# Each indirect row transfer waits for the one before it, and three pairs of a scatter move behind the group norm's root

## The chip, the cores and the metric

One core of one Trainium2 chip. The metric is device microseconds of one execution. Before the change it is 2342.63 us, the median of 3 runs (2340.99 to 2352.11).

## The reference, cut to what matters

Eight images of 128 channels by 32 by 32 (1024 tokens of 128 channels each) go through four layers, each added to its input:

```
x = x + deform_conv(_gn(x))               # layer 0: 3x3 deformable convolution
x = x + attention_conv(_gn(x))            # layer 1: softmax attention over 1024 positions
t = tokens(x)
t = t + attention(_ln_t(t))               # layer 2: softmax attention with a distance bias
t = t + top2_experts(_ln_t(t), weights a) # 8 experts, hidden 256, each token uses 2
t = t + linear_attention(_ln_t(t))        # layer 3
t = t + top2_experts(_ln_t(t), weights b)
```

`_gn` is a group norm over 4 channels and all positions, `_ln_t` a layer norm over a token's 128 channels; both divide by a square root. The expert layer adds, for each token, the outputs of its two best experts with their shares.

## The kernel before, in words

Five engines run programs that are written out image by image. While image p is in its convolution and its two attentions, the expert layers and layer 3 of images p-1, p-2 and p-3 are woven in at numbered hooks; tables such as `SEND_A_AT` give the hook of every step. The hooks of the convolution and of the short stage behind it are numbered 0 to 52 (`G_HOOKS`), those of the two attentions start again at 0 (`X_HOOKS`). An engine runs its own list strictly in order and waits on semaphores, so on GpSimd, which does nothing but small work, a table decides only what stands before what.

The expert layer of an image works on sorted rows. After routing, GpSimd **scatters** the 1024 normed tokens twice (first and second choice) into `xs` in device memory: 16 indirect transfers (`MOVES`), each of 128 rows of 512 bytes, out of `tnF` (first expert layer, l = 0) or `tnB` (second, l = 1). `send(m, l, part)` issues two of them. SyncE's `first_blocks` asks for the first six weight blocks, then waits until all 16 have landed (`sent0` or `sent1`, 256 counts an image) and loads `xs` into `blocks_sb` in three pieces (L689). TensorE turns these blocks over four at a time (L1101, step 0 of `experts`), works through 23 blocks, and SyncE stores the results to `ys`. Then GpSimd **gathers** them back in 16 indirect transfers into `gotten` (`fetch`), and VectorE's `settle` (L1829), which waits for all 16 (`got0` or `got1`), adds them to the tokens.

GpSimd also takes every norm's root (`rsqrt`, `rsqrt_half`: variance to the power -0.5). Each sits between a VectorE step that makes the variance and one that uses the root: `gn0` and `gn1` are the group norms before the convolution and before the first attention, `ln2` the norm before the second attention, `lnf2` and `lnf3` those before the expert layers, `ln3` that before layer 3. `ln2`, `lnf2` and `lnf3` go in two halves of four token tiles. One larger piece, the sum `tokD + tnB` at L785, is GpSimd's too.

So in one period GpSimd's list holds, in this order: the gather of l = 0 for image p-1; the `ln3` root and half a `lnf2` root; four transfers of the gather of l = 1 for image p-3, the other `lnf2` half, L785, and the other twelve; the scatter of l = 0 for image p-1, the `lnf3` halves and the `gn1` root among it; the scatter of l = 1 for image p-2 with the first `ln2` half ahead of its last two transfers. After the last image's convolution there is a tail of hooks with the same steps and nothing else to weave them into; there the last image's expert layers are computed densely, without transfers.

Of the kernel before, what the change touches and what calls it, by code (L numbers as in the profile page):

```python
# [73 lines left out]
def placed(first, at, hooks):  # L74

    return [[first + n for n, h in enumerate(at) if h == hook] for hook in range(hooks)]
# [23 lines left out]
LAYER3_PLACES = placed(EARLY_LAYER3, LAYER3_AT, G_HOOKS)  # L100
GATE_A_AT = [1, 4, 4, 4, 7, 8, 8, 10, 13, 17, 17, 21, 21, 22]
GATE_A_PLACES = placed(EARLY_GATING, GATE_A_AT, G_HOOKS)
SEND_A_AT = [28, 32, 34, 34, 36, 36, 44, 44]
SEND_A_PLACES = placed(0, SEND_A_AT, G_HOOKS)
GATE_B_AT = [36, 42, 43, 43, 45, 46, 46, 46, 46, 51, 51]
GATE_B_PLACES = placed(0, GATE_B_AT, G_HOOKS)
# [171 lines left out]
def at(m, k, c):  # L278

    reg, off = m  # L280
    return off * k + c if reg is None else reg * k + (off * k + c)


def later(value):

    return not isinstance(value, int) or value > 0
# [12 lines left out]
def build(nc, x, sel_in, count_in, early_in, late_in, wa_in, wb_in, out):  # L299
# [3 lines left out]
    with ExitStack() as ctx:  # L303
# [5 lines left out]
        def sem(name):  # L309
            if name not in sems:  # L310
                sems[name] = ctx.enter_context(nc.semaphore(name))
            return sems[name]
# [52 lines left out]
        got = [gotten[:, r * N:(r + 1) * N].rearrange("p (a b) -> p a b", a=NT) for r in range(2)]  # L365
# [89 lines left out]
        def which(l):  # L455

            return ("lnf2", "lnf3")[l], "ab"[l], "FB"[l], (tnF, tnB)[l], (tnTA, tnTB)[l]

        def nth(m, l, k, c):

            i, v = m
            if l == 0:
                return c if i is None and v == 0 else at(m, 2 * k, c - k)
            return at(m, 2 * k, c + 2 * k if v + 1 < B - 1 else c + k)

        def before_this(m, l, k):

            i, c = m
            if l == 0:
                return at(m, k, -k)  # L470
            return at(m, k, 2 * k) if c + 1 < B - 1 else (B - 1) * k
# [7 lines left out]
        def there(p, n):  # L479

            return not isinstance(p, int) or 0 <= p - n < B
# [23 lines left out]
        def tail_side(rear, layer3, gating, send, first_blocks, experts, fetch, settle, load, dense):  # L505

            def side(n):
                for (thread, l, age), places in TAIL_PLACES.items():
                    m = None, B - 1 - age
                    for step in places[n]:  # L510
                        if thread == "rear":
                            rear(m, step)
                        elif thread == "layer3":
                            layer3(m, step)
                        elif thread == "gating":
                            gating(m, l, step)
                        elif thread == "send":
                            send(m, l, step)
                        elif thread == "first":
                            first_blocks(m, l)  # L520
                        elif thread == "experts":
                            experts(m, l, step)
                        elif thread == "fetch":
                            fetch(m, l, step)
                        elif thread == "settle":
                            settle(m, l, step)
                        elif thread == "load":
                            load(l)
                        else:
                            dense(m, l, step)  # L530
            return side
# [46 lines left out]
        def periods(period, tail):  # L578

            for p in range(B):  # L580
                period((None, p), p)
            for n in range(X_HOOKS, TAIL_HOOKS):
                tail(n)
# [169 lines left out]
        @block.gpsimd  # L753
        def _(pool):
            pool.memset(mhalf[:, :], -0.5).then_inc(sem("mhalf_set"), 1)
            pool.memset(prob[:, :], 0.0)
            pool.drain().then_inc(sem("prob_zero"), 1)
            pool.memset(xrows[:, :], 0.0)
            pool.drain().then_inc(sem("pads_zero"), 1)
            pool.wait_ge(sem("mhalf_set"), 1)  # L760

            def rsqrt_half(m, w, name, h):
                pool.wait_ge(sem(name + "_var"), at(m, 2, h + 1))
                cols = slice(4 * h, 4 * h + 4)
                pool.tensor_tensor(stat[w]["rstd"][:, cols], stat[w]["var"][:, cols], mhalf[:, cols],
                                   ALU.pow).then_inc(sem(name + "_rstd"), 1)

            def rsqrt(m, w, name, width):
                pool.wait_ge(sem(name + "_var"), at(m, 1, 1))
                pool.tensor_tensor(stat[w]["rstd"][:, 0:width], stat[w]["var"][:, 0:width], mhalf[:, 0:width],  # L770
                                   ALU.pow).then_inc(sem(name + "_rstd"), 1)

            def gating(m, l, step):
                name, f, w, tn, tnT = which(l)
                for h in range(2):
                    if step == GATE_AT[h][POWER]:
                        rsqrt_half(m, w, name, h)

            def layer3(m, step):
                if step == 2:  # L780
                    rsqrt(m, "B", "ln3", NT)
                elif step == 7:

                    pool.wait_ge(sem("ln3_tn"), at(m, 2, 2))
                    pool.tensor_tensor(tokD[:, :, :], tokD[:, :, :], tnB[:, :, :], ALU.add).then_inc(sem("tok3_res"), 1)  # L785

            MOVES = [(r, j) for r in range(2) for j in range(NT)]

            def send(m, l, part):

                if part == 0:
                    pool.wait_ge(sem(f"routed{l}"), at(m, 1, 1))
                    pool.sem_inc(sem("moves_begun"), 1)
                tn = which(l)[3]
                for r, j in MOVES[2 * part:2 * part + 2]:
                    pool.indirect_dma_start(xs[l], bass.IndirectOffsetOnAxis(row[l][r][:, j:j + 1], 0), tn[:, j, :], None)\  # L796
                        .then_inc(sem(f"sent{l}"), 16)

            def fetch(m, l, part):

                if part == 0:
                    if later(before_this(m, l, 1)):
                        pool.wait_ge(sem(f"settled{1 - l}"), before_this(m, l, 1))
                    for y in range(STORES):
                        pool.wait_ge(sem(f"ys_out{y}"), 16 * nth(m, l, 2, 2))
                    pool.sem_inc(sem("moves_begun"), 1)
                for r, j in MOVES[2 * part:2 * part + 2]:
                    pool.indirect_dma_start(got[r][:, j, :], None, ys[l], bass.IndirectOffsetOnAxis(row[l][r][:, j:j + 1], 0))\  # L808
                        .then_inc(sem(f"got{l}"), 16)

            def rear(m, step):
                if step < MOVE_STEPS:
                    fetch(m, 1, step)

            def start(m, step):
                if step == 5:
                    rsqrt(m, "S", "gn0", 1)

            tail = tail_side(rear, layer3, gating, send, nothing, nothing, fetch, nothing, nothing, nothing)

            def period(m, p):
                side = g_sides(m, p, rear, layer3, gating, send, nothing, nothing)
                for n in range(G_HOOKS):
                    if there(p, 0) and n == CONV_HOOKS + 5:
                        rsqrt(m, "F", "gn1", 1)
                    side(n)
                side = x_sides(m, p, layer3, gating, send, nothing, nothing, fetch, nothing, start, tail)
                for n in range(X_HOOKS):
                    if there(p, 0) and n in (ATTENTION_HOOKS - 5, ATTENTION_HOOKS + 4):
                        rsqrt_half(m, "F", "ln2", n // ATTENTION_HOOKS)  # L830
                    side(n)

            rsqrt((None, 0), "S", "gn0", 1)
            pool.wait_ge(sem("xs_zero"), 64)


            periods(period, tail)
# [1329 lines left out]
```

## Time and profile before

| | |
|---|---|
| median of 3 runs | 2342.63 us |
| span of the profiled execution | 2532.1 us |
| TensorE busy | 1926.7 us, 76% |
| VectorE busy | 1494.0 us, 59% |
| ScalarE busy | 1039.0 us, 41% |
| GpSimd busy | 555.5 us, 22%, 535 instructions, 448 of them indirect transfers |

The profiled execution is known by its span alone, the time from its first to its last instruction; it is 8% above the median of the runs. The rows quoted further down are times within it, so what is summed there has to be brought to the scale of the runs by 2342.63 / 2532.1 = 0.925. A transfer's own instruction on GpSimd ends when its descriptors are written, not when its rows have landed.

### The profile page before, as it was taken

To read this page: it belongs to the slowest core of one execution; us is meant where nothing else is said; L and a number is where in the kernel's file an instruction comes from. 1 tells how busy PE (TensorE), PEld (TensorE's weight loads), DVE (VectorE), ACT (ScalarE), POOL (GpSimd) and SP (SyncE) were. 2 spreads that over 40 slices of the span, in tenths; PEclk is the share of its full clock that TensorE was granted. 3 is DMA by queue.
4 is the path that set the end of the run, shared out by engine and by line. 5 is a ranking of instruction groups with operands and counts; after the bars stand their busy time and mean duration, and the time that the engine had idled before them with its cause. 6 is when DMAs were issued, how large, how long until landed. Compare 5 with 4: busy or idle time off the path is not lost.

```text
span 2532.1 us, 35891 instructions
## 1 busy us (share of the span) xinstructions
PE 1926.7 (76%) x10992; PEld 1518.5 (60%) x10992; DVE 1494.0 (59%) x3449; ACT 1039.0 (41%) x1773; POOL 555.5 (22%) x535
## 2 busy tenths in 40 slices
PE   4777878887688777877778876786778877768749
PEld 1665656566556565756646665565656666556636
DVE  2356545876357754777447763577547864485363
ACT  3134144525363162733546253642627335443323
POOL 0000112021213323032222312133230422232020
PEclk7889989988899889988889888998889988888969
DMA  7901952474446734584455844476344844431410
GB/s 250 198 1 42 210 150 76 110 170 136 123 137 162 199 101 127 146 184 142 117 145 158 187 138 122 135 178 182 101 132 146 192 132 126 128 122 55 129 35 9
DMA packets 259912, 337.51 MB, mean 133 GB/s; under 512 B 29552, under 2 KB 191840, under 8 KB 259424
## 3 DMA queue, kind: packets, MB, share of 16 engines
q1 hardware_dynamic: 243648, 297.70, 44.7%
q0 software_dynamic: 14336, 29.39, 4.2%
q10 hardware_dynamic: 1696, 7.66, 0.8%
q8 instruction: 105, 1.72, 0.3%
q14 instruction: 127, 1.04, 0.1%
HBM read 267.56 MB, written 67.08 MB: 132 GB/s over the span
## 4 chain that ended last, share of the span: by engine, by line
PE 33%; issue 19%; DVE 18%; ACT 6%; DVEq 5%; DMA 5%; SPq 4%; another core or an unknown queue 4%; POOL 3%; ACTq 2%; PEld 0%; PEldq 0%; POOLq 0%
PE pair L948 5%; PE pair L1067 4%; POOL gotten L808 2%; PE pair L935 2%; PE pair L1235 2%; PE pair L1225 2%; PE pair L1115 2%; DMA dist<-hats 2%; PE pair L1127 2%; PE pair L1075 2%; DVE dist L1642 2%; PE pair L861 2%; PE pair L881 2%; DVE nmax L1751 1%
## 5 line engine op out<-in xcount | busy, mean ns | idle before, releaser
L948 PE MATMUL pair<-dist,thirds 128*128 128x256 f32 (+6 forms) x1440 | 299.2, 360 | 66.7 <-DVE dist L1642 60.7
L948 PEld LDWEIGHTS pair<-dist,thirds 128*128 128x128 f32 x1440 | 259.5, 205 | 115.3 <-DVE dist L1642 61.2
L1067 PE MATMUL pair<-vt,dist 128*128 128x128 f32 x2048 | 270.7, 288 | 37.3 <-DVEq L1745 32.9
L1067 PEld LDWEIGHTS pair<-vt,dist 128*128 128x128 f32 x2048 | 256.2, 202 | 60.5 <-DVEq L1745 49.8
L1433 ACT ACTIVATE hidden_sb<-pair,wring 128x128 f32<-128x128 f32 x644 | 184.3, 367 | 234.8 <-PE pair L1115 135.2
L808 POOL DMA_INDIRECT gotten<-ys,row x224 | 226.0, 1009 | 128.1 <-issue 65.8
L1115 PE MATMUL pair<-turned_sb,wring 128*128 128x128 f32 x1288 | 193.1, 295 | 65.1 <-DVEq L1796 37.2
L1127 PE MATMUL pair<-wring,hidden_sb 128*128 128x128 f32 x1288 | 184.5, 288 | 71.6 <-DVE tnF L1764 35.9
L1115 PEld LDWEIGHTS pair<-turned_sb,wring 128*128 128x128 f32 x1288 | 172.8, 205 | 106.6 <-DVEq L1796 61.9
L1642 DVE TENSOR_TENSOR dist<-dist,prob 128x1024 f32<-128x1024 f32 x144 | 173.9, 1224 | 95.7 <-DMA dist<-hats 46.9
L1127 PEld LDWEIGHTS pair<-wring,hidden_sb 128*128 128x128 f32 x1288 | 169.3, 202 | 81.7 <-issue 65.8
L1751 DVE TENSOR_REDUCE nmax<-pair 128x1 f32<-128x1024 f32 x128 | 156.6, 1224 | 50.0 <-PE pair L1075 35.0
L796 POOL DMA_INDIRECT xs<-tnB,row x112 | 108.9, 973 | 322.6 <-DVEq L1927 290.1
L796 POOL DMA_INDIRECT xs<-tnF,row x112 | 126.5, 1130 | 236.9 <-DVEq L1927 164.1
L1405 ACT ACTIVATE prob<-pair,nmax 128x1024 f32<-128x1024 f32 x128 | 142.4, 1113 | 83.7 <-DVE nmax L1751 73.0
L1340 ACT ACTIVATE thirds<-pair 128x768 f32<-128x768 f32 x96 | 77.8, 810 | 239.1 <-PE pair L935 220.9
L935 PE MATMUL pair<-early_sb,xrows 128*128 128x384 f32 x384 | 152.7, 522 | 24.1 <-ACT thirds L1340 15.4
L1059 PE MATMUL pair<-early_sb,prob 128*128 128x128 f32 x1024 | 150.6, 280 | 20.0 <-ACT hidden_sb L1433 7.7
L1808 DVE TENSOR_TENSOR by<-pair,wring 128x256 f32<-128x256 f32 x168 | 69.2, 412 | 160.3 <-PE pair L1127 79.3
L1393 ACT ACTIVATE dist<-pair 128x512 f32<-128x512 f32 x128 | 76.3, 596 | 168.0 <-PE pair L1059 98.9
L1059 PEld LDWEIGHTS pair<-early_sb,prob 128*128 128x128 f32 x1024 | 122.0, 145 | 33.7 <-issue 12.2
L1075 PE MATMUL pair<-qk 128*128 128x512 f32 x256 | 130.2, 634 | 9.6 <-issue 6.1
(256 smaller groups left out, 3162.0 us busy)
## 6 DMA issues: line engine op xcount, KB each, us to landing
dist<-hats SPq DMA_DIRECT2D x576, 128.0 KB
wring<-wa SPq DMA_DIRECT2D x161, 321.0 KB
wring<-wb SPq DMA_DIRECT2D x161, 321.0 KB
prob<-hats SPq DMA_DIRECT2D x288, 128.0 KB
hats<-dist SPq DMA_DIRECT2D x40, 512.0 KB, 3.9
ys<-by SPq DMA_DIRECT2D x70, 256.0 KB, 2.3
blocks_sb<-xs SPq DMA_DIRECT2D x28, 512.0 KB, 6.7
blocks_sb<-xs SPq DMA_DIRECT2D x14, 448.0 KB, 8.0
```

What stands on the lines that cost most here:

```text
L796: pool.indirect_dma_start(xs[l], bass.IndirectOffsetOnAxis(row[l][r][:, j:j + 1], 0), tn[:, j, :], None)\
L808: pool.indirect_dma_start(got[r][:, j, :], None, ys[l], bass.IndirectOffsetOnAxis(row[l][r][:, j:j + 1], 0))\
L935: last = pe.matmul(pair[1][:, 512 * c:512 * c + 384], xn[:, (2 * d + c) * P:(2 * d + c + 1) * P], const("w0")[:, t * 384:(t + 1) * 384], s ...
L948: last = pe.matmul(pair[0][:, a:b], z[k // 3 % 2][:, c, k % 3, :], rhs(a, b), start=bank not in opened, stop=final, skip_group_check=True)
L1059: last = pe.transpose(psum[bank][:, t * P:(t + 1) * P], pr[j % 3][:, (4 * h + t) * P:(4 * h + t + 1) * P], ident)
L1067: last = pe.matmul(psum[bank][:, 0:P], prT[j % 2][:, t, :], vt[:, t, :], start=(t == 0), stop=(t == NT - 1))
L1075: last = pe.matmul(pair[j % 2][:, h * 512:(h + 1) * 512], queries[:, j * P:(j + 1) * P], keys[:, h * 512:(h + 1) * 512], start=True, stop= ...
L1115: last = pe.matmul(psum[bank][:, to:to + P], wring[:, r, h * P:(h + 1) * P], bT[b0 // 4 % 2][:, (b % 4) * P:(b % 4 + 1) * P], start=True, ...
L1127: last = pe.matmul(psum[bank][:, to:to + P], hid[b % 4][:, h * P:(h + 1) * P], wring[:, b % RINGW, W2_AT + h * C:W2_AT + (h + 1) * C], sta ...
L1433: last = act.activation(hid[b % 4][:, h * P:(h + 1) * P], psum[bank][:, of:of + P], ACT.Gelu, bias=wring[:, b % RINGW, B1_AT + h:B1_AT + h ...
L1642: dve.tensor_tensor(slot, slot, windows(k, half), ALU.mult).then_inc(sem("hat_ready"), 1)
L1751: dve.tensor_reduce(nmax[:, j:j + 1], pair[j % 2][:, :], AX.X, ALU.max, negate=True)\
```

## The change

Every indirect transfer but the first of a batch of 16 gets a wait: for all 16 counts of every transfer issued before it in its batch. The wait is carried by the transfer's own instruction. Nothing else is computed or moved, but the table `SEND_A_AT` puts the last three pairs of the scatter of l = 0 at hooks 46, 47 and 48 where they had 36, 44 and 44; the `gn1` root stands at hook 45.

```diff
-SEND_A_AT = [28, 32, 34, 34, 36, 36, 44, 44]
+SEND_A_AT = [28, 32, 34, 34, 36, 46, 47, 48]
...
-                for r, j in MOVES[2 * part:2 * part + 2]:
+                for n, (r, j) in enumerate(MOVES[2 * part:2 * part + 2]):
+                    if part or n:
+
+                        pool.wait_ge(sem(f"sent{l}"), at(m, 256, 32 * part + 16 * n))
                     pool.indirect_dma_start(xs[l], bass.IndirectOffsetOnAxis(row[l][r][:, j:j + 1], 0), tn[:, j, :], None)\
                         .then_inc(sem(f"sent{l}"), 16)
...
-                for r, j in MOVES[2 * part:2 * part + 2]:
+                for n, (r, j) in enumerate(MOVES[2 * part:2 * part + 2]):
+                    if part or n:
+
+                        pool.wait_ge(sem(f"got{l}"), at(m, 256, 32 * part + 16 * n))
                     pool.indirect_dma_start(got[r][:, j, :], None, ys[l], bass.IndirectOffsetOnAxis(row[l][r][:, j:j + 1], 0))\
                         .then_inc(sem(f"got{l}"), 16)
```

Only GpSimd's list changes. Its rows for the end of a convolution, before (`xs<-tnF` is the scatter of l = 0, `xs<-tnB` that of l = 1; xN is a run of N equal rows):

```order
L796 DMA xs<-tnF,row 2944x128 [waits routed0]
L796 DMA xs<-tnF,row 2944x128 x11
L765 TENSOR_TENSOR rstdB<-varB,mhalf 128x4 [waits lnf3_var]
L796 DMA xs<-tnF,row 2944x128 x4
L770 TENSOR_TENSOR rstdF<-varF,mhalf 128x1 [waits gn1_var]
L765 TENSOR_TENSOR rstdB<-varB,mhalf 128x4 [waits lnf3_var]
L796 DMA xs<-tnB,row 2944x128 [waits routed1]
```

And the same place in the changed kernel:

```order
L799 DMA xs<-tnF,row 2944x128 [waits routed0]
L799 DMA xs<-tnF,row 2944x128 [waits sent0] x9
L765 TENSOR_TENSOR rstdB<-varB,mhalf 128x4 [waits lnf3_var]
L770 TENSOR_TENSOR rstdF<-varF,mhalf 128x1 [waits gn1_var]
L765 TENSOR_TENSOR rstdB<-varB,mhalf 128x4 [waits lnf3_var]
L799 DMA xs<-tnF,row 2944x128 [waits sent0] x6
L799 DMA xs<-tnB,row 2944x128 [waits routed1]
```

Two of the twelve scatters ahead of the first `lnf3` half and the four ahead of the `gn1` root now stand behind both, and, since the second `lnf3` half comes right after the `gn1` root, behind that too.

GpSimd's rows for the start of a convolution, where the gather of l = 1 begins (`-` before, `+` changed):

```order
 L765 TENSOR_TENSOR rstdF<-varF,mhalf 128x4 [waits lnf2_var]
-L808 DMA gotten<-ys,row 128x128 [waits ys_out2,ys_out1,settled0,ys_out0]
-L808 DMA gotten<-ys,row 128x128 x3
+L814 DMA gotten<-ys,row 128x128 [waits ys_out2,ys_out1,settled0,ys_out0]
+L814 DMA gotten<-ys,row 128x128 [waits got1] x3
 L765 TENSOR_TENSOR rstdF<-varF,mhalf 128x4 [waits lnf2_var]
 L785 TENSOR_TENSOR tokD<-tokD,tnB 128x1024 [waits ln3_tn]
-L808 DMA gotten<-ys,row 128x128 x12
```

Here nothing changes places: the second `lnf2` half and the sum at L785 stand behind four transfers as before, and three of these four now wait.

## Rows read from the trace of the kernel before

**Rows 1.** The page: engines, their busy time, share of the span and instructions.
```profile
PE 1926.7 (76%) x10992; PEld 1518.5 (60%) x10992; DVE 1494.0 (59%) x3449; ACT 1039.0 (41%) x1773; POOL 555.5 (22%) x535
```
**Rows 2.** Timeline of POOL, fifth period: start, length, operation [idle before, releaser].
```profile
1136.20 1.44 POOL L796 DMA_INDIRECT xs<-tnF,row  x1 [30.43 <-DVEq L1927]
...
1152.39 0.97 POOL L796 DMA_INDIRECT xs<-tnF,row  x1 [0.30 <-issue]
1161.65 1.03 POOL L765 TENSOR_TENSOR rstdB<-varB,mhalf 128x4 f32<-128x4 f32 x1 [8.29 <-DVE varB L1692]
...
1171.20 0.57 POOL L770 TENSOR_TENSOR rstdF<-varF,mhalf 128x1 f32<-128x1 f32 x1 [3.47 <-DVEq L1575]
1174.43 1.01 POOL L765 TENSOR_TENSOR rstdB<-varB,mhalf 128x4 f32<-128x4 f32 x1 [2.66 <-DVE varB L1692]
```
**Rows 3.** Timeline of SP (issues of transfers): the fifth period, and the tail.
```profile
1173.85 3.92 SPq L689 DMA_DIRECT2D blocks_sb<-xs  x3
...
2344.46 2.18 SPq L689 DMA_DIRECT2D blocks_sb<-xs  x3
```
**Rows 4.** Timeline of PE, the same place of the fifth period.
```profile
1187.03 0.60 PE L1101 MATMUL pair<-early_sb,blocks_sb 128*128 128x128 f32 x4
```
**Rows 5.** The tile blocks_sb: its loads, from issue to landing, in us.
```profile
DMA to landing us min/median/max: 3.9/7.2/9.2
```
**Rows 6.** DMA queues in 2342.15:2344.15, 1301.3:1303.6 and 1376.2:1385.5: packets, MB, share.
```profile
q0 software_dynamic: 64, 0.13, 19.5%
...
q0 software_dynamic: 64, 0.13, 22.8%
...
q0 software_dynamic: 128, 0.26, 14.1%
```
**Rows 7.** Timeline of DVE: four instructions that make or use what POOL waits for.
```profile
1135.01 0.34 DVE L1926 TENSOR_REDUCE row<-picked 128x8 int32<-128x64 f32 x2
...
1256.99 0.17 DVE L1692 TENSOR_SCALAR varF<-mvF 128x4 f32<-128x4 f32 x1
...
1260.19 0.16 DVE L1701 SCALAR_TENSOR_TENSOR nmrF<-mvF,rstdF 128x4 f32<-128x4 f32 x1
...
1385.64 2.33 DVE L1701 SCALAR_TENSOR_TENSOR nmrF<-mvF,rstdF 128x4 f32<-128x4 f32 x1
```
**Rows 8.** Timeline of POOL: the first ln2 root, fifth period and last image.
```profile
1257.25 1.04 POOL L765 TENSOR_TENSOR rstdF<-varF,mhalf 128x4 f32<-128x4 f32 x1 [21.59 <-DVE varF L1692]
...
2138.53 1.04 POOL L765 TENSOR_TENSOR rstdF<-varF,mhalf 128x4 f32<-128x4 f32 x1 [11.34 <-DVE varF L1692]
```
**Rows 9.** Timeline of POOL: the gather of l = 1 begins, then the second lnf2 root.
```profile
1376.23 1.01 POOL L808 DMA_INDIRECT gotten<-ys,row  x1 [0.18 <-issue]
...
1384.59 1.02 POOL L765 TENSOR_TENSOR rstdF<-varF,mhalf 128x4 f32<-128x4 f32 x1 [3.51 <-DVE varF L1692]
```
**Rows 10.** Timeline of POOL: the first transfer of four more gathers.
```profile
418.51 1.03 POOL L808 DMA_INDIRECT gotten<-ys,row  x1 [0.18 <-issue]
...
1281.42 1.03 POOL L808 DMA_INDIRECT gotten<-ys,row  x1 [9.14 <-DMA ys<-by]
...
2244.90 1.12 POOL L808 DMA_INDIRECT gotten<-ys,row  x1 [0.18 <-issue]
...
2414.53 1.03 POOL L808 DMA_INDIRECT gotten<-ys,row  x1 [11.24 <-DMA ys<-by]
```
**Rows 11.** Timeline of DVE: the first use of each of these four gathers.
```profile
448.17 0.61 DVE L1829 SCALAR_TENSOR_TENSOR tokD<-gotten,share,tokD 128x128 f32<-128x128 f32 x2
...
1325.07 0.61 DVE L1829 SCALAR_TENSOR_TENSOR tokD<-gotten,share,tokD 128x128 f32<-128x128 f32 x2 [0.21 <-issue]
...
2277.39 1.72 DVE L1829 SCALAR_TENSOR_TENSOR tokC<-gotten,share,tokC 128x128 f32<-128x128 f32 x5
...
2442.78 0.35 DVE L1829 SCALAR_TENSOR_TENSOR xc<-gotten,share,xc 128x128 f32<-128x128 f32 x1
```
**Rows 12.** Groups of DVE: line, operation, count | busy, mean ns | idle before, releasers.
```profile
L1642 DVE TENSOR_TENSOR dist<-dist,prob 128x1024 f32<-128x1024 f32 x144 | 173.9, 1224 | 95.7 <-DMA dist<-hats 46.9 <-DMA prob<-hats 38.2 <-issue 8.1
```

## The prediction

> **What bounds the kernel now.** The page's first part comes first: TensorE is busy for 76% of the span and no engine comes near all of it [rows 1], so the kernel is bound by the order in which in-order engines hand work to each other, and a wait costs what it holds up. GpSimd is idle for most of the span; its load is not the question, but what stands behind its transfers is. So I read its timeline, and for each batch of 16 transfers looked for the next thing that needs it. Three things are to be seen there. A scatter goes out every 1.27 us (0.97 us long after 0.30 us idle) and GpSimd then idles 8.29 us before the first `lnf3` root, so its transfers are paid for by nobody [rows 2]. Behind the scatter of l = 0 the slack is small: SyncE issues the loads of `blocks_sb` at 1173.85 [rows 3] and TensorE turns the first block over at 1187.03 [rows 4], of which the load takes 3.9 us at best [rows 5]. And most gathers have room: one begins at 1281.42 [rows 10] and is first used at 1325.07 [rows 11].
>
> **What one waited transfer costs.** It takes the landing of the one before plus the wake of GpSimd.
>
> The landing, with the DMA engines otherwise idle: a window of 2.0 us that begins with the issue of a batch's last scatter holds all 64 packets of the last two transfers, 0.13 MB [rows 6], and SyncE, which waits for this landing, goes on at 2344.46 [rows 3]: 1.9 us, and 0.4 us for SyncE's start. The same for a gather: a window of 2.3 us, 2.2 us taken. Beside other loads: the four gathers from 1376.2 have all 128 packets moved by 1385.5, 9.3 us [rows 6]. One alone lies between 9.3 / 4 = 2.3 us and 9.3 - 3 x 1.3 = 5.4 us; I take 3.7 us, near the middle. For scatters beside some load I take 2.3 us.
>
> The wake does not show, since no transfer carries a wait today. Bound from below: a norm's root, which carries its own wait, starts 0.09 us after the variance is made (1256.99 + 0.17 [rows 7] to 1257.25 [rows 8]). Bound from above: a batch's first transfer stands behind an instruction that only waits and counts, and starts 0.85 us after routing's last write (1135.01 + 0.34 [rows 7] to 1136.20 [rows 2]). Nearest in kind is the 0.30 us between two transfers, same engine and operation; with 0.07 us more for the semaphore I take 0.37 us. A waited transfer then costs 2.27 us (scatter, idle), 2.67 us (scatter, some load), 2.57 us (gather, idle) or 4.07 us (gather, loaded), against 1.27 us.
>
> On the wake the Trainium skill has a rule (Perfetto Trace Analysis, DMA Instruction — SWDGE (GPSIMD)): such an instruction is decoded first, sits in a wait queue, and moves to the processors once its semaphores are satisfied, so a wait that it carries costs no decoding afterwards. By that rule the wake is near the lower bound and the sum is that of the first rival below; no row here shows it for a transfer.
>
> **The change part by part, in us of the profiled execution.**
>
> 1. Scatter of l = 0, seven periods. The `gn1` root at 1171.20 and the second `lnf3` root, which ends at 1174.43 + 1.01 [rows 2], keep their places, 4.24 us apart; 0.2 us later six scatters start where the four before them had gone out already. They land 5 x 2.27 + 1.9 = 13.25 us on, SyncE starts 0.4 us later and the first piece takes 3.9 us (DMA is idle by then): 4.24 + 0.2 + 13.25 + 0.4 + 3.9 = 22.0 us behind the `gn1` root, against 15.83 us for TensorE's first turn now (1187.03 - 1171.20). TensorE is in order, VectorE and ScalarE wait for that block: **6.2 us late, 43 us in seven periods**. With the median landing of 7.2 us [rows 5] it would be 23 us more. That the last three pairs come behind the root is what keeps the `gn1` root on time: the ten scatters ahead of it have 1171.20 - 1136.20 = 35.0 us, enough up to (35.0 - 2.4) / 9 = 3.6 us each.
>
> 2. Scatter of l = 1. Thirteen waits lie ahead of the first `ln2` root: 13 x (2.67 - 1.27) = 18.2 us. GpSimd idles 21.59 us there now [rows 8], so it is hidden, in all images but the last, whose idle time is 11.34 us [rows 8]. VectorE reads the root 1.9 us after it is there (1260.19 [rows 7] against 1257.25 + 1.04): 18.2 - 11.3 - 1.9, **5 us once**.
>
> 3. Gather of l = 0. It lasts 15 x 2.57 + 2.2 = 40.8 us. The room is 43.65 us (1281.42 [rows 10] to 1325.07 [rows 11]), in six periods about the same: hidden, with 2.9 us left. In the first it is 29.66 us (418.51 to 448.17 [rows 10, 11]): **11 us once**.
>
> 4. Gather of l = 1, five periods. Three waits stand ahead of the second `lnf2` root: 3 x (4.07 - 1.3) = 8.3 us, against 3.51 us idle [rows 9]. VectorE takes that root the moment it ends (1384.59 + 1.02, then 1385.64 [rows 7]), so it is 4.8 us late. But this is where the convolution starts, in which VectorE waits for loads, 46.9 + 38.2 us in all, 10.6 us an image [rows 12]; loads that go on while it is held shorten those waits. Between nothing and all I take half: 2.4 x 5, **12 us**. The other twelve have the whole convolution.
>
> 5. Tail. Here nothing is woven in and the engines work in chains. The gather at 2244.90 takes fifteen waits, three of them loaded, with a root (1.0) and the L785 sum (2.3, as long as VectorE's 1385.64 beside it [rows 7]) in between: 3 x 4.07 + 12 x 2.57 + 2.2 + 3.3 = 48.6 us, to 2293.5, used now at 2277.39: 16 us. The last one, 40.8 us from 2414.53, ends at 2455.3 and is used now at 2442.78 [rows 10, 11]: 12.5 us; two `lnf3` roots and the last image's last layer follow it. **28.5 us.**
>
> Sum: 43 + 5 + 11 + 12 + 28.5 = 99.5 us on a span of 2532.1 us. The runs are shorter by the factor 0.925, so 92 us on the median of 2342.63: **2435 us**.
>
> **The rivals.**
>
> *Short wake* (0.09 us, 0.28 us less a transfer; the Trainium skill's rule above stands behind it). Parts 1 to 5 fall to 34, 1.4, 7, 10 and 20: 72 us, times 0.925 = 67, **2409 us**. For it speaks the root's 0.09 us; against it the constant 0.30 us between transfers.
>
> *Long wake* (0.85 us, 0.48 us more). Part 1 gives 60; part 2 11 in the last image and 0.9 in five others; part 3 18 in the first period and 7.2 - 2.9 = 4.3 in six others, half of it counted since TensorE has queued work in the second attention, so 31; part 4 16; part 5 43: 166 us, times 0.925 = 153, **2496 us**. For it speaks the only transfer in the trace that follows a wait.
>
> *Overrun.* If scatters beside the convolution's loads cost as much as gathers there, 3.7 + 0.85 us, they pass the 3.6 us of part 1 and the `gn1` root is 9 x 0.95 = 8.6 us late in six periods, 51 us more; with the halves of parts 3 and 4 counted whole (28 us): 245 us, times 0.925, **2569 us**.
>
> *Hidden.* The waits cost nothing if the six scatters behind the root land in time: (1187.03 - 3.9 - 0.4 - 1175.64 - 1.9) / 5 = 1.04 us each, less than a landing [rows 6] and even than today's 1.27 us. It could be only if runs without a profiler land far faster: **2343 us**.
>
> *Faster.* Twelve scatters now go out in 17 us beside the loads VectorE waits for in the convolution [rows 12]; ten spread out, and six behind it, leave these loads more room. If that halves the waits (42.5 us) and part 1 is hidden as above: 2342.63 - 39 = **2303 us**. It decides only where a waited scatter costs at most 1.04 us.
>
> **How the numbers follow.** A measurement of this kernel tells about 0.5% from no change. Forecast (wake 0.37 us) 0.47, long wake 0.26, short wake 0.16, overrun 0.05, hidden 0.04, faster 0.02. Slower is the sum of the first four, 0.94; same 0.04, faster 0.02. The range goes from under the short wake's time, 2385 us (absorption as in part 4 may reach part 1 too), to the long wake's, 2500 us; outside are overrun, hidden, faster and some of the edges, less than 2 in 10.
>
> **What would show it.** In the changed profile a scatter should start every 2.3 to 2.7 us and a gather every 2.6 to 4.1 us, with idle time ended by a landing; the first L1101 rows (there L1107) should lie 22 us behind the `gn1` root and be waited for; the `gn1` root's own wait should be no longer than now; L1829 (there L1835) should wait for `gotten` in the first period and twice in the tail. I am wrong if the starts lie 2.0 or 2.8 us apart (the wake), if TensorE's first turn is not held up, or if the convolution gives back more than half of what the `lnf2` root loses.

## The result, and the profile after

The changed kernel takes 2786.7 us (median of 4 runs, 2774.07 to 2798.88), and the kernel before took 2345.07 us beside it (4 runs): a ratio of 1.189, 95% interval 1.185 to 1.193. That is 442 us slower, against 92 us forecast and an upper end of 2500 us. The direction was right, the size was not.

The page of the changed kernel: the engines' busy time, the row of the queue of indirect transfers (packets, MB, share), and the chain that ended last.

```profile
PE 1925.9 (69%) x10992; PEld 1518.1 (55%) x10992; DVE 1495.2 (54%) x3449; ACT 1039.8 (37%) x1773; POOL 558.9 (20%) x535
...
q0 software_dynamic: 14336, 29.39, 3.8%
...
DMA 49%; issue 17%; PE 14%; DVE 8%; SPq 3%; POOL 3%; ACT 2%; DVEq 2%; ACTq 1%; PEld 0%; POOLq 0%; PEldq 0%
DMA gotten<-ys,row 25%; DMA xs<-tnF,row 11%; DMA xs<-tnB,row 9%; PE pair L1073 2%; PE pair L1121 2%; PE pair L1241 1%; PE pair L1231 1%; DMA blocks_sb<-xs 1%; DMA ys<-by 1%; PE pair L954 1%; DMA prob<-hats 1%; DVE nmax L1757 1%; DVE dist L1750 1%; PE pair L941 1%; PE pair L1081 1%
```

Every engine runs the same instructions as before [rows 1], and the span is longer. That TensorE's busy time equals the one in [rows 1] is no sign that its speed is unchanged: the second profile of the unchanged kernel, further down, has 1876.3 us for the same 10992 matmuls, at a mean granted clock of 0.907 against 0.849 here and 0.883 in the first. The clock has two levels in these traces, 2.4 GHz (1.00) and 1.2 GHz (0.50). At the turn of the first block below, behind 8.65 us without work, the four matmuls run at 0.50 and take 1.11 us, against 0.60 us at 1.00 in [rows 4]. So the waits also made TensorE's own work 50 us longer; no run holds the clock fixed, so what part of the loss this is stays open.

The chain is half DMA, and 25 + 11 + 9 = 45% of the span are landings of indirect transfers, on a queue that moves data for 3.8% of it. So the loss comes from latency, not from bandwidth.

Who waits is in the view of waits: engine, tile and line <- releaser: us in total, times, longest.

```profile
POOL gotten L814 <- DMA gotten<-ys,row: 522.7, 203, 7.4
...
POOL xs L799 <- DMA xs<-tnF,row: 208.7, 98, 7.0
...
POOL xs L799 <- DMA xs<-tnB,row: 195.1, 104, 4.8
...
DVE tokD L1835 <- DMA gotten<-ys,row: 137.3, 7, 24.4
DVE nmrF L1707 <- POOL rstdF L765: 130.1, 26, 18.6
...
PE pair L1107 <- DMA blocks_sb<-xs: 77.6, 8, 19.6
...
DVE tokC L1835 <- DMA gotten<-ys,row: 56.4, 6, 16.4
...
DVE dist L1648 <- DMA prob<-hats: 45.0, 17, 4.7
...
DVE dist L1648 <- DMA dist<-hats: 40.4, 26, 12.6
...
DVE xc L1835 <- DMA gotten<-ys,row: 21.1, 1, 21.1
...
DVE nmrB L1707 <- POOL rstdB L765: 15.6, 7, 5.6
DVE nmrF L1584 <- POOL rstdF L770: 15.2, 8, 10.1
```

GpSimd's own waits (first three rows, 926 us) are not the loss by themselves; it is only 442 us. What costs are three waits of the others: VectorE's for `gotten` (137.3 + 56.4 + 21.1 = 214.8 us), VectorE's for a root behind the transfers (the `nmr` rows), and TensorE's for `blocks_sb` (77.6 us). The waits for the `hats` loads are as in [rows 12], so the loads gave nothing back there.

The timeline of GpSimd in the period that answers to [rows 2, 8, 10]: the end of a scatter of l = 0, a scatter of l = 1 with its `ln2` root, and the gather of l = 0.

```profile
1261.36 0.97 POOL L799 DMA_INDIRECT xs<-tnF,row  x1 [2.37 <-DMA xs<-tnF,row]
1262.36 1.04 POOL L765 TENSOR_TENSOR rstdB<-varB,mhalf 128x4 f32<-128x4 f32 x1
1265.19 0.56 POOL L770 TENSOR_TENSOR rstdF<-varF,mhalf 128x1 f32<-128x1 f32 x1 [1.79 <-DVEq L1581]
...
1269.60 1.03 POOL L799 DMA_INDIRECT xs<-tnF,row  x1 [0.19 <-issue]
...
1284.02 0.96 POOL L799 DMA_INDIRECT xs<-tnF,row  x1 [1.56 <-DMA xs<-tnF,row]
...
1320.73 0.96 POOL L799 DMA_INDIRECT xs<-tnB,row  x1 [35.76 <-DVEq L1933]
...
1358.72 0.96 POOL L799 DMA_INDIRECT xs<-tnB,row  x1 [1.54 <-DMA xs<-tnB,row]
1361.21 0.96 POOL L799 DMA_INDIRECT xs<-tnB,row  x1 [1.54 <-DMA xs<-tnB,row]
1362.20 1.03 POOL L765 TENSOR_TENSOR rstdF<-varF,mhalf 128x4 f32<-128x4 f32 x1
...
1384.15 1.03 POOL L814 DMA_INDIRECT gotten<-ys,row  x1 [6.83 <-DMA ys<-by]
...
1433.20 0.94 POOL L814 DMA_INDIRECT gotten<-ys,row  x1 [1.89 <-DMA gotten<-ys,row]
```

The view of the chain tells landing and wake apart (start, length, what; "issue" is the time from the landing to the start that waited for it), at the end of that scatter of l = 1, and between the last landing of the scatter of l = 0 and SyncE:

```profile
1356.23 2.23 DMA xs<-tnB,row
1358.45 0.27 issue
...
1286.27 0.02 issue
```

Three readings. The price of a waited transfer: on a quiet queue scatters start 2.49 us apart (1358.72 to 1361.21), of which 2.23 are the landing and 0.27 the wake. The forecast had 1.9 and 0.37. It had split what it saw wrongly: it set 0.4 us aside for SyncE's start, and SyncE starts 0.02 us behind the landing. The idle time ahead of the `ln2` root, 21.59 us in [rows 8], is gone: the root starts the moment its engine is done with the thirteenth waited scatter. And the gather of l = 0 takes 49.05 us from its first start to its last, 3.27 us a step on the average.

SyncE's timeline behind the scatter of l = 0 (compare [rows 3]):

```profile
1286.29 1.95 SPq L689 DMA_DIRECT2D blocks_sb<-xs  x3
```

TensorE's, there and behind the tail's scatter of l = 1 (compare [rows 4]):

```profile
1290.44 1.11 PE L1107 MATMUL pair<-early_sb,blocks_sb 128*128 128x128 f32 x4 [8.65 <-DMA blocks_sb<-xs]
...
2596.32 1.11 PE L1107 MATMUL pair<-early_sb,blocks_sb 128*128 128x128 f32 x4 [19.60 <-DMA blocks_sb<-xs]
```

VectorE's uses of the first `ln2` root, and of the second `lnf2` root of the next convolution (compare [rows 7]):

```profile
1363.26 0.16 DVE L1707 SCALAR_TENSOR_TENSOR nmrF<-mvF,rstdF 128x4 f32<-128x4 f32 x1 [14.07 <-POOL rstdF L765]
...
1499.52 2.31 DVE L1707 SCALAR_TENSOR_TENSOR nmrF<-mvF,rstdF 128x4 f32<-128x4 f32 x1 [4.77 <-POOL rstdF L765]
```

From the start of a scatter's last transfer until SyncE goes on it takes 2.27 us (1284.02 to 1286.29), as forecast (1.9 + 0.4), though nearly all of it is landing. The waits in which the forecast saw nothing are those of 14.07 us (scatter of l = 1) and of about 20 us for `tokD` (gather of l = 0, 137.3 us in seven).

### The profile page after: what moved, and what is told of

It is laid out like the page before. It is cut to its first block, busy times and chain, and to the rows that moved or that the text cites. A ratio compares the mean times of both kernels' runs of the same rounds, so it can differ in the third digit from the quotient of the medians.

```text
span 2784.9 us, 35891 instructions
## 1 busy us (share of the span) xinstructions
PE 1925.9 (69%) x10992; PEld 1518.1 (55%) x10992; DVE 1495.2 (54%) x3449; ACT 1039.8 (37%) x1773; POOL 558.9 (20%) x535
## 3 DMA queue, kind: packets, MB, share of 16 engines
q0 software_dynamic: 14336, 29.39, 3.8%
q8 instruction: 105, 1.72, 0.3%
## 4 chain that ended last, share of the span: by engine, by line
DMA 49%; issue 17%; PE 14%; DVE 8%; SPq 3%; POOL 3%; ACT 2%; DVEq 2%; ACTq 1%; PEld 0%; POOLq 0%; PEldq 0%
DMA gotten<-ys,row 25%; DMA xs<-tnF,row 11%; DMA xs<-tnB,row 9%; PE pair L1073 2%; PE pair L1121 2%; PE pair L1241 1%; PE pair L1231 1%; DMA blocks_sb<-xs 1%; DMA ys<-by 1%; PE pair L954 1%; DMA prob<-hats 1%; DVE nmax L1757 1%; DVE dist L1750 1%; PE pair L941 1%; PE pair L1081 1%
## 5 line engine op out<-in xcount | busy, mean ns | idle before, releaser
L954 PE MATMUL pair<-dist,thirds 128*128 128x256 f32 (+6 forms) x1440 | 305.3, 364 | 82.3 <-DVE dist L1648 76.0
L954 PEld LDWEIGHTS pair<-dist,thirds 128*128 128x128 f32 x1440 | 263.2, 207 | 137.3 <-DVE dist L1648 80.5
L1073 PEld LDWEIGHTS pair<-vt,dist 128*128 128x128 f32 x2048 | 262.0, 206 | 57.2 <-DVEq L1751 45.0
L1133 PE MATMUL pair<-wring,hidden_sb 128*128 128x128 f32 x1288 | 174.5, 279 | 26.6 <-DVE tokA L1772 24.6
L1133 PEld LDWEIGHTS pair<-wring,hidden_sb 128*128 128x128 f32 x1288 | 161.4, 195 | 32.7 <-issue 27.7
L901 PE MATMUL pair<-early_sb,tnF 128*128 128x128 f32 x192 | 36.8, 323 | 138.4 <-DVEq L1711 138.4
```

What stands on the lines that cost most here:

```text
L954: last = pe.matmul(pair[0][:, a:b], z[k // 3 % 2][:, c, k % 3, :], rhs(a, b), start=bank not in opened, stop=final, skip_group_check=True)
L1073: last = pe.matmul(psum[bank][:, 0:P], prT[j % 2][:, t, :], vt[:, t, :], start=(t == 0), stop=(t == NT - 1))
L1133: last = pe.matmul(psum[bank][:, to:to + P], hid[b % 4][:, h * P:(h + 1) * P], wring[:, b % RINGW, W2_AT + h * C:W2_AT + (h + 1) * C], sta ...
```

## The experiments

Two theories were at hand. **A**: the rooms that the prediction read for the scatter of l = 1 and the gather of l = 0 belonged to the one profiled execution, whose span lay 8% above the runs, and are much smaller in an ordinary one; the loss is then the sum of the three waits above, batch by batch. **B**: the rooms are there, and something else costs, the moved pairs or each wait as such.

**The kernel before, unchanged, profiled again.**

> The kernel before, unchanged, profiled a second time. The profiled execution of before had a span of 2532.1 us against 2343 us for its runs, and in it all three compute engines stand still together five times for 9 to 12 us while a scatter of l = 1 is issued and three times for 4 to 6 us during a gather of l = 0. Theory A (standstills of that one execution, absent from the runs): span near 2345 us, no such standstill, and the room of a gather of l = 0 (first transfer to first use) near 33 us instead of 43.65 us, that of the scatter of l = 1 ahead of the ln2 root near 29 us instead of 39.15 us. Theory B (the profiler stops the engines whenever 14 to 16 transfers go out back to back): span near 2530 us again, standstills at the same places. Theory C (the standstills belong to the kernel and the runs have them too): the span and the runs of this call agree near 2530 us.

2343.17 us, ratio 1.001 (0.998 to 1.004); the profiled span is 2337.8 us. GpSimd's timeline in the same place as above:

```profile
1156.48 1.03 POOL L796 DMA_INDIRECT xs<-tnB,row  x1 [42.88 <-DVEq L1927]
...
1173.09 0.97 POOL L796 DMA_INDIRECT xs<-tnB,row  x1 [0.30 <-issue]
1181.62 1.04 POOL L765 TENSOR_TENSOR rstdF<-varF,mhalf 128x4 f32<-128x4 f32 x1 [7.56 <-DVE varF L1692]
...
1206.02 1.03 POOL L808 DMA_INDIRECT gotten<-ys,row  x1 [9.37 <-DMA ys<-by]
...
1288.60 1.01 POOL L808 DMA_INDIRECT gotten<-ys,row  x1 [0.18 <-issue]
```

VectorE's use of that root, and its first uses of the gathers of l = 0 and of l = 1:

```profile
1184.56 0.17 DVE L1701 SCALAR_TENSOR_TENSOR nmrF<-mvF,rstdF 128x4 f32<-128x4 f32 x1
...
1237.42 0.61 DVE L1829 SCALAR_TENSOR_TENSOR tokD<-gotten,share,tokD 128x128 f32<-128x128 f32 x2 [0.20 <-issue]
...
1345.08 1.98 DVE L1829 SCALAR_TENSOR_TENSOR tokC<-gotten,share,tokC 128x128 f32<-128x128 f32 x6
```

Here the idle time ahead of the root is 7.56 us, not 21.59, and the room of the gather is 1237.42 - 1206.02 = 31.4 us, not 43.65. Its view of waits has VectorE wait 26.3 us for roots, most of it in this row:

```profile
DVE nmrF L1701 <- POOL rstdF L765: 18.3, 15, 2.3
```

The first profile had the difference as standstills of all three computing engines in just these places: set side by side instruction by instruction, VectorE's timelines of the two profiles differ by 194 us at the end, and about 175 of them arise beside a scatter of l = 1 or a gather of l = 0. Its windows view (length, busy time and count of TensorE, its weight loads, VectorE, ScalarE and GpSimd, clock, DMA share, GB/s) there:

```profile
1226.00:1238.00 12.00, 0.36 (x1) 0.19 (x1) 0.00 (x0) 0.00 (x0) 7.53 (x8) 0.63 0.37 110
```

VectorE's timeline at the ends of two such stretches:

```profile
1238.10 0.16 DVE L1761 RECIPROCAL rinv<-rsum 128x1 f32<-128x1 f32 x1 [13.80 <-remote]
...
1303.20 0.42 DVE L1808 TENSOR_TENSOR by<-pair,wring 128x256 f32<-128x256 f32 x1 [12.86 <-remote]
```

In 12 us GpSimd started eight scatters while TensorE, VectorE and ScalarE together ran one matmul and its weight load. The releaser reads "remote": nothing that the profile records ended the wait. The second standstill, before 1303.20, lies within the gather of l = 0. A standstill gives the batch under way time in which nothing that needs it comes nearer; the second profile has no stretch of over 3 us without work on these three engines, but for the loads at its start. Theory A holds for the rooms. The expectation's other two are out: a profile does not always hold standstills, and the runs, at 2343 us, do not have them.

**The move alone, and the waits alone.** The order of pairs without the waits, and the waits with the order of before:

```diff
-SEND_A_AT = [28, 32, 34, 34, 36, 36, 44, 44]
+SEND_A_AT = [28, 32, 34, 34, 36, 46, 47, 48]
```

> Kernel before with the table of the change alone (three pairs of the scatter of l = 0 behind the gn1 root), no waits. Theory A (the loss is the waits): six transfers 1.27 us apart behind the second lnf3 root land about 8.3 us after it, TensorE's first turn is 0 to 2 us late in seven periods, less than four transfers' time earlier: between 2335 and 2360 us. Rival (the move itself holds up the blocks): 40 us or more, 2385 us.

2356.65 us, ratio 1.005 (1.003 to 1.008): 13 us. The waits view has one new row for it:

```profile
PE pair L1101 <- DMA blocks_sb<-xs: 10.8, 6, 2.9
```

> The changed kernel with the old table: every transfer waits, and the last four scatters of l = 0 stand ahead of the gn1 root. Theory A: twelve, then four waited scatters at 2.5 to 3 us each hold the first lnf3 root and the gn1 root up by 5 to 15 us, while the blocks land earlier behind the root; what is lost ahead of the root is about what is won behind it: 2760 to 2830 us. Rival (the move is what costs): under 2700 us.

2816.18 us (2 runs), ratio 1.202 (1.195 to 1.210), 29 us more than the changed kernel. Both runs came out in theory A's range. So the table costs 13 us by itself, and given the waits it saves about 30: it takes six waited scatters from ahead of the `gn1` root (VectorE's wait for that root is 74.2 us with the old table and 15.2 with the new), two of them from ahead of the first `lnf3` root (56.6 and 15.6 us).

**One batch at a time.** The changed kernel with waits in one kind of batch only; the first is shown, in the other three the condition stands on the other l or in `fetch`:

```diff
-                    if part or n:
+                    back_ = 2 * part + n - 1
+                    if back_ >= 0 and (l == 0):
-                        pool.wait_ge(sem(f"sent{l}"), at(m, 256, 32 * part + 16 * n))
+                        pool.wait_ge(sem(f"sent{l}"), at(m, 256, 16 * back_ + 16))
```

> Edit: the changed kernel with the waits in the scatter of l = 0 alone; the new table stays. Theory A (the waits cost what TensorE, VectorE and the loads are seen to wait for in the changed kernel's trace, batch by batch): TensorE's seven waits for blocks_sb are 7.1 to 9.2 us, 58 us together, and the table by itself costs 12: 2343 + 70 = 2413 us (2400 to 2425). Theory B (the sums of the prediction, with the slack read in the profile of before that had standstills): 43 x 0.925 + 12 = 52, 2395 us. The two are near each other here, because no slack of a standstill goes into this part.

2438.07 us, ratio 1.044 (1.040 to 1.048), +97 us.

> Edit: waits in the scatter of l = 1 alone; the new table stays. Theory A: in an undisturbed run of before GpSimd idles 7.6 us ahead of the first ln2 root, not 21.6, and thirteen waits lengthen what lies ahead of it by 24 us, so the root is late by 12 to 14 us in each of six periods, and TensorE waits 19.6 us in the tail: about 101 us and 12 for the table, 2456 us (2435 to 2465). Theory B (hidden but in the last image, 5 us): 2343 + 5 + 12 = 2360 us.

2477.84 us, ratio 1.059 (1.055 to 1.063), +137 us.

> Edit: waits in the gather of l = 0 alone; the new table stays. Theory A: the room is 31 us, not 43.65, and the waited batch takes 51, so VectorE waits 18 to 24 us for gotten in each of seven periods, 137 us together, of which 86 are time in which TensorE and ScalarE stand still too: 86 to 137 and 12 for the table, 2441 to 2492 us. Theory B (hidden but in the first period, 11 us): 2343 + 10 + 12 = 2365 us, up to 2373 with the longer wake that was measured.

2498.08 us, ratio 1.067 (1.062 to 1.071), +157 us.

> Edit: waits in the gather of l = 1 alone; the new table stays. Theory A: VectorE waits 7 to 9 us for gotten in five periods, 40 us, then 16.5 and 21.1 in the tail, and the second lnf2 root is 4.8 us late five times: about 100 us and 12 for the table, 2455 us (2435 to 2465). Theory B (parts 4 and 5 as predicted, 40.5 x 0.925, and no wait for gotten in the five periods): 2343 + 37 + 12 = 2392 us. If the four parts add up, the four runs less four times the table are 429 us, what the changed kernel has over the table; if waits of one batch take the place of another's, the four give more than that.

2468.62 us, ratio 1.054 (1.049 to 1.059), +128 us.

The waits that carry these stand in the view of waits. Waits in the scatter of l = 0 alone:

```profile
PE pair L1109 <- DMA blocks_sb<-xs: 59.9, 8, 9.1
...
DVE nmrB L1709 <- POOL rstdB L765: 20.5, 6, 5.4
```

In the scatter of l = 1 alone:

```profile
DVE nmrF L1709 <- POOL rstdF L765: 108.1, 21, 19.1
...
PE pair L1109 <- DMA blocks_sb<-xs: 31.6, 7, 21.8
```

In the gather of l = 0 alone:

```profile
DVE tokD L1837 <- DMA gotten<-ys,row: 145.4, 7, 23.6
```

In the gather of l = 1 alone:

```profile
DVE tokC L1837 <- DMA gotten<-ys,row: 55.1, 6, 16.3
```

B's numbers for scatter l = 1, gather l = 0 and gather l = 1 (2360, 2365, 2392) miss by 118, 133 and 77 us; A's middles lie 14 to 25 us low in three of four, and all four times are above the upper end of A's range, by 4 to 13 us. So A has the mechanism, and its sizes are a little short. What A missed in scatter l = 0 is the 20.5 us row: the first `lnf3` root stands behind nine waited scatters, which take longer beside the convolution's loads than room is there. The four less four times the table's 13 us are 520 - 52 = 468 us, 9% more than the changed kernel's 442 - 13 = 429: the batches' costs nearly add up, and a little of one's lateness also serves another.

**Two in flight.** Each transfer waits for the one two before it, on two semaphores in turn; SyncE and VectorE then wait for both.

```diff
-                    if part or n:
-                        pool.wait_ge(sem(f"sent{l}"), at(m, 256, 32 * part + 16 * n))
+                    i = 2 * part + n
+                    if i >= 2:
+                        pool.wait_ge(sem(f"sent{l}_{i % 2}"), at(m, 128, 16 * (i // 2)))
...
-                        .then_inc(sem(f"sent{l}"), 16)
+                        .then_inc(sem(f"sent{l}_{i % 2}"), 16)
```

> Each transfer waits for the one two before it in its batch, counted on two semaphores in turn, so that two may be under way; table of the change. Theory A (the price is landing plus wake, 1.9 + 0.62 = 2.5 us for a scatter and 2.2 + 0.62 = 2.8 us for a gather, now spread over two): a transfer every 1.3 to 1.5 us, nearly the 1.27 us of before, 2345 to 2390 us. Rival (each waited instruction costs its own wake and cannot be issued ahead): a step of at least 1.0 + 0.62 = 1.6 us or more, 2450 us or more.

2382.27 us, ratio 1.017 (1.013 to 1.021): 38 us, not 442. This is in theory A's range, and the rival's 2450 us or more is out. (The 0.62 us in this expectation and in that of the wait apart is 2.49 less a landing of 1.9; the sum is right, and the chain view above divides it into 2.23 and 0.27.)

> Edit: each transfer waits for the one two before it (two semaphores in turn, as in the run two back), with the order of pairs of before. Theory A: with two in flight the twelve scatters ahead of the gn1 root still have room, and only four instead of six stand behind it, so TensorE's waits for blocks_sb (0.7 to 2.9 us a period with the new table) go: 12 to 15 us less than two back with the new table, 2365 us (2355 to 2375). Theory B (the waits make the roots late where twelve scatters stand ahead, as with one in flight, where the old table cost 30 us): 2382 + 5 to 30, 2387 to 2412 us.

2358.84 us, ratio 1.006 (1.003 to 1.008): by the ratios some 25 us less than with the new table, in A's range; B had the other sign. With two in flight the order of before is the better one again: by the view of waits TensorE's for `blocks_sb` fall from 14.1 us to one of 2.3 us.

**Half the waits.** Only the first transfer of a pair waits, in scatters and gathers alike.

```diff
-                    if part or n:
+                    if part and not n:
```

> Edit: the changed kernel, but only the first transfer of each pair waits (for both of the pair before); the second goes out at once: half the waits, the new table. Theory A (room against length, batch by batch, with the rooms of an undisturbed run): a pair takes 1.27 + 2.5 = 3.8 us for scatters and 4.05 for gathers, some load on top; the gather of l = 0 lasts about 35 us against 31 of room (26 us in seven periods), the ln2 root is 1.5 late (9), TensorE's blocks about 4.5 late (31), tail 24: about 90 us, 2435 us (2405 to 2450). Theory B (the loss goes with the number of waits): half of the 431 us that the waits cost, and 12 for the table, 2570 us.

2484.43 us, ratio 1.058 (1.051 to 1.066), +139 us. B's rule that the loss goes with the number of waits (2570) falls: half the waits leave under a third of it. A's sum was 49 us low, since a pair beside other loads took longer than the 3.8 to 4.05 us and little extra that I put in: the `gotten` waits are 61.4 us (26 expected), roots 36.7 over before (9), `blocks_sb` 43.2 (31 and the tail). These three sum to 141 us, what was measured.

**The wait on an instruction of its own.** In scatters and gathers alike:

```diff
                         pool.wait_ge(sem(f"sent{l}"), at(m, 256, 32 * part + 16 * n))
+                        pool.sem_inc(sem("apart"), 1)
                     pool.indirect_dma_start(xs[l], ...
```

> Edit: the changed kernel; each of the 420 waits stands on a GpSimd instruction of its own (it counts a semaphore up that nobody waits for) just ahead of its transfer, instead of on the transfer. Theory A (a carried wait saves the start of the transfer): the step from transfer to transfer grows by about 0.85 - 0.62 = 0.2 to 0.3 us, 13 to 15 times in nearly every one of 28 batches whose end something waits for now: 70 to 95 us, 2786 + 70 to 95 = 2855 to 2880 us, and the start lies about 0.85 us behind the landing. Theory B (the 0.62 us is the way of the semaphore alone, and the transfer starts at once behind it either way): within 10 us of 2787, steps unchanged at 2.49 us in the quiet part of the scatter of l = 1.

2955.74 us, ratio 1.262 (1.253 to 1.270), 169 us over the changed kernel. The quiet step is 3.00 us here (723.48 to 726.48), 2.49 there, by the view of the chain in a scatter of l = 1 (POOLq is GpSimd's sequencer with the counting instruction):

```profile
723.48 2.21 DMA xs<-tnB,row
725.70 0.02 issue
725.72 0.02 POOLq L799
725.74 0.74 issue
```

B is out. A had the sign and the start, which is 0.78 us behind the landing (0.85 expected), but half the size: the carried wake is 0.27 us and not 0.62, so the step grows by 0.51 us instead of 0.2 to 0.3. GpSimd's waits grow by 176 us (from 926 to 1103), and the time by 169; 420 transfers of 0.51 us more are 214 us. So at this point about four fifths of what the transfers take longer is paid, while of the first 926 us of waits less than half was: the rooms are nearly used up.

**One tally for all.** For each run, the three waits of its trace (VectorE for `gotten`, VectorE for roots less the 26.3 us that the kernel before has, TensorE for `blocks_sb`) beside the time over the kernel before:

| kernel | `gotten` | roots | `blocks_sb` | sum, us | measured, us |
|---|---|---|---|---|---|
| move only | 0 | 0.1 | 10.8 | 11 | 13 |
| two back, old table | 3.2 | 13.9 | 2.3 | 19 | 13 |
| two back | 6.1 | 5.9 | 14.1 | 26 | 38 |
| scatter l = 0 | 0 | 27.5 | 59.9 | 87 | 97 |
| gather l = 1 | 75.7 | 16.2 | 9.0 | 101 | 128 |
| scatter l = 1 | 0 | 89.5 | 31.6 | 121 | 137 |
| pairs | 61.4 | 36.7 | 43.2 | 141 | 139 |
| gather l = 0 | 145.4 | -0.3 | 11.5 | 157 | 157 |
| changed kernel | 214.8 | 135.4 | 77.6 | 428 | 442 |
| waits, old table | 209.2 | 239.0 | 22.1 | 470 | 472 |
| wait apart | 291.3 | 209.0 | 97.0 | 597 | 610 |

Over losses from 13 to 610 us the tally is within 27 us everywhere and within 16 in all but one. The largest miss, 27 us in the gather of l = 1, lies in part with TensorE's clock: in that run TensorE is busy for 1907.6 us, against 1876.3 in the second profile of before, and VectorE waits 21.9 us for the matmuls that `lga` is made from, against 11.7. The windows view (columns as above, the clock third from the end) over the same eight of these matmuls, in that run and in the second profile of before:

```profile
1053.35:1055.07 1.72, 1.72 (x10) 1.72 (x9) 0.00 (x0) 0.00 (x0) 0.68 (x1) 0.50 0.08 24
...
1031.56:1032.51 0.95, 0.95 (x10) 0.94 (x9) 0.21 (x2) 0.37 (x1) 0.57 (x1) 1.00 0.99 184
```

That the clock makes up all of the 27 us is not shown.

## Why the prediction was wrong, step by step

**The frame was right.** The waits cost what they hold up on other engines, the short waits on GpSimd itself nothing; the change lost time; no rival of the other sign came true. By the tally's three waits the five parts cost 82, 115, 137, 56 and 37.5 us, against 43, 5, 11, 12 and 28.5 forecast.

**The step that failed is "hidden" in parts 2 and 3.** Both rested on a room read in one execution: 21.59 us ahead of the `ln2` root [rows 8] and 43.65 us ahead of `tokD` [rows 10, 11]. That execution was 8% longer than the runs, and the factor 0.925 spread the 8% evenly over the kernel, though nearly all of it sat in these two places. The unchanged kernel, profiled again, has 7.56 and 31.4 us. The one room that the prediction read as short, 29.66 us in the first period [rows 10, 11], is what all seven periods have there (26.4 to 32.7 us). Part 2 measured 115 us (the 130.1 us row less 18.3 before and less 16.2 of part 4's root, and 19.6 in the tail) and part 3 137, against 5 and 11 forecast. Of these 252 us the right rooms with the forecast's own step give 18.2 - 7.56 - 1.9 = 8.7 us in six periods and 40.8 - 31.4 = 9.4 us in seven, 118 us. The rest is the step: thirteen waited scatters take 40.48 us instead of 16.61 (1320.73 to 1361.21, 1156.48 to 1173.09), 23.9 more and not 18.2, and the gather 51.6 us with its last landing of 2.5, not 40.8. What was too small in the step is the landing: 2.2 to 5.5 us in that scatter, where 2.3 was taken, and 2.5 to 4.0 us in that gather, where the 2.2 of a quiet queue was taken. With rooms and steps both as measured the two come to (23.9 - 7.56 - 1.9) x 6 + 19.6 in the tail + 20.2 x 7 = 248 us.

**The wake was not what made it long.** It is 0.27 us, 0.10 shorter than forecast. The quiet scatter's landing is 2.23 us where 1.9 was taken, so its step is 2.49 and not 2.27, and beside loads the landing grows further. No row shows the term of 0.4 us for SyncE's start; it is 0.02. The rivals by mechanism: *short wake* needs a start within 0.1 us of the landing; *long wake* needs 0.85 us, which only the run with the wait apart comes near (0.78), so if its 2496 us had come out, that would have been luck; *hidden* needs landings near 1 us; none of this is there. *Overrun* did happen, but small (the roots of part 1 cost 24 us, not 51): at the first `lnf3` root, and at the `gn1` root in the first period alone. *Faster* asked the `hats` waits to halve; they are 45.0 + 40.4 us, as they were.

The Trainium skill's rule that such an instruction is decoded first and then waits in a queue until its semaphores are satisfied (Perfetto Trace Analysis, DMA Instruction — SWDGE (GPSIMD)) holds as far as the two runs go: a wait that the transfer carries saves 0.5 us over one ahead of it. The 0.09 us that the prediction read out of the rule is too short: the start comes 0.27 us behind the landing.

**Part 1**, 6.2 us seven times (43), measured 58 us for `blocks_sb` (77.6 less 19.6 in the tail), 7.1 to 9.2 each, and 24 us in roots. In the fifth period TensorE turns the block over 1290.44 - 1265.19 = 25.3 us behind the `gn1` root, forecast 22.0: its five waited steps take 14.4 us (1269.60 to 1284.02), not 11.35. The sentence that ten scatters ahead of the `gn1` root have room was right for that root in all periods but the first (its longest wait, 10.1 us), but missed the first `lnf3` root ahead of it, which now starts the moment the tenth scatter is out (1262.36, no idle time; 8.29 us in [rows 2]).

**Part 4** had the root exactly: 4.77 us late at 1499.52, 4.8 forecast. The half that the convolution was to give back: 16.2 us over before in the run with the gather of l = 1 alone, 12 forecast. But "the other twelve have the whole convolution" was wrong by the prediction's own price of a loaded gather: 15 x 4.07 + 2.2 + 3.3 = 66.6 us, and the unchanged kernel has 1345.08 - 1288.60 = 56.5 us from its first transfer to its first use. The trace has 7 to 9 us of `tokC` wait in each of five periods, 40 us that the sum lacked.

**Part 5** was 28.5; the two gathers cost 16.4 + 21.1 = 37.5. Not seen was the tail's scatter of l = 1, 19.6 us at 2596.32.

## What to carry to other kernels

Compare the span of a profiled execution with the runs before reading slack from it; where it is some per cent longer, find where the extra time sits (stretches in which all computing engines stand still), since slack next to it is not there in an ordinary run, and a common factor does not mend it. A wait for each landing turns sixteen overlapped latencies into a sum; it costs nothing until a batch outgrows its room and then nearly all of it, so forecast each batch as length less room, with the landing taken beside the loads that really go on there. If transfers must be held back, let two be in flight on two semaphores: that cost 0.6% here with the order of before and 1.7% with the moved pairs, where one in flight costs 19%.

## What the runs showed of the hardware

- An indirect transfer that carries its wait starts 0.27 us after the landing it waits for, 0.78 us when the wait stands on the instruction ahead; the quiet steps are 2.49 and 3.00 us, against 1.27 without waits.
- SyncE goes on 0.02 us after the landing it waits for (1286.27 to 1286.29).
- The transfers move 29.39 MB in 448, 65.6 KB each. By the fit of the Trainium skill (DMA: Bandwidth & Descriptors, Anatomy of one DMA — SWDGE (gpsimd) path), 2.0 us plus the bytes at 436 GB/s, that is an estimated 2.15 us each; on a quiet queue the trace has 2.2 us for a scatter and 2.5 for a gather, so it agrees within 0.4 us. The page calls most of it latency of completion; the runs with two in flight, in which most of it is overlapped, fit that.
- TensorE runs the same eight matmuls in 0.95 us at a granted clock of 1.00 and in 1.72 us at 0.50. Its mean granted clock is 0.907 in the second profile of before, 0.849 in the changed kernel and 0.832 with the wait apart.
- Standstills of 4 to 12 us in which TensorE, VectorE and ScalarE all wait while GpSimd goes on starting transfers, in one profiled execution of the unchanged kernel and not in the second. What causes them, no row shows, and no run was made to provoke them; it stays open.
